# Slot transfers issued by piece, high pieces first, and the mask's halves exchanged behind them

## What is computed

```
x = x + L0_xattn(layernorm(x), ctx)        # 16 heads of width 8, rotary, no mask
x = x + L0_ffn(layernorm(x))               # ternary weights
x = x + L1_xattn(layernorm(x), ctx, mask)  # 16 query heads, 4 key heads, causal AND mask
x = x + L1_ffn(layernorm(x))               # 8 experts, the best one for each token
```

## Time and profile before

| | us |
|---|---|
| median of 3 runs | 588.3 (587.66 to 589.43) |
| the profiled execution, its own time | 586.95 |
| its span | 585.1 |
| PE busy in the span | 495.1 (85%) |
| DVE / ACT / POOL busy | 399.3 / 357.0 / 374.8 |

### The profile page before, as it was taken

One profiled execution on the slowest core, in us unless ns is written; L12 is line 12 of the kernel. 1 busy time (PEld: TensorE's weight loads), 2 busy tenths in 40 slices (PEclk: granted clock), 3 DMA queues, 4 the chain that ended last, 5 costly groups with the idle time before them and its releaser, 6 DMA issues.

```text
span 585.1 us, 20027 instructions
## 1 busy us (share of the span) xinstructions
PE 495.1 (85%) x6238; PEld 363.5 (62%) x6239; DVE 399.3 (68%) x1244; ACT 357.0 (61%) x872; POOL 374.8 (64%) x751
## 2 busy tenths in 40 slices
PE   3569898999988799988799999899998742999993
PEld 2346566666665589986455555555554422999992
DVE  7657777777798568644668888888878763444441
ACT  3227677777766555653566777677765652666661
POOL 6876666667673257675666688878887472445552
PEclk9999999999999999999999999999999985999998
DMA  5734334353432580004443455444554014334430
GB/s 165 184 76 125 90 92 118 85 126 87 119 89 64 193 226 1 1 2 111 118 111 89 104 134 137 128 103 111 133 138 110 26 56 143 80 96 104 101 94 27
DMA packets 102161, 59.92 MB, mean 102 GB/s; under 512 B 20338, under 2 KB 98178, under 8 KB 102098
## 3 DMA queue, kind: packets, MB, share of 16 engines
q1 hardware_dynamic: 98738, 51.79, 35.1%
q0 software_dynamic: 2784, 6.82, 3.4%
q10 hardware_dynamic: 576, 0.53, 0.3%
HBM read 19.90 MB, written 8.81 MB: 49 GB/s over the span
## 4 chain that ended last, share of the span: by engine, by line
PE 47%; SPq 14%; DVE 10%; DMA 10%; issue 10%; ACT 4%; POOL 3%; ACTq 1%; DVEq 0%; POOLq 0%
SPq L395 8%; DMA stack<-pieces 7%; PE bank L847 6%; PE bank L783 5%; PE bank L669 5%; PE scoreT L773 4%; DVE negmax L1408 4%; PE scoreT L835 4%; PE score L613 4%; PE bank L556 2%; PE score L835 2%; SPq L404 2%; PE bank L528 2%; PE scoreT L642 2%; PE bank L684 2%
## 5 line engine op out<-in xcount | busy, mean ns | idle before, releaser
L1408 DVE TENSOR_REDUCE negmax<-score 128x8 f32<-128x1024 f32 x128 | 156.2, 1220 | 35.4 <-PE score L613 24.9
L956 ACT ACTIVATE P<-scoreT 128x1024 f32<-128x1024 f32 x128 | 131.0, 1023 | 40.1 <-PE scoreT L633 21.7
L669 PE MATMUL bank<-P,Vc 128*32 128x128 f32 x2048 | 82.5, 279 | 1.9 <-DVE product L1516 1.5
L613 PE MATMUL score<-stack 64*128 64x128 bf16 x1024 | 62.7, 222 | 22.1 <-DMA stack<-pieces 13.1
L1312 POOL DMA_INDIRECT out<-by x39 | 40.2, 1031 | 50.6 <-DVE by L1715 48.0
L613 PEld LDWEIGHTS score<-stack 64*128 64x128 bf16 x1024 | 33.9, 95 | 48.7 <-issue 22.1
L669 PEld LDWEIGHTS bank<-P,Vc 128*32 128x32 f32 x2048 | 48.4, 109 | 15.8 <-issue 3.6
L962 ACT COPY outs<-bank 128x256 f32<-128x256 f32 x64 | 23.6, 369 | 49.8 <-PE bank L669 49.6
L1176 POOL TENSOR_TENSOR pieces<-full,pieces 128x256 bf16<-128x256 f32 x64 | 42.9, 670 | 14.4 <-ACT pieces L937 14.4
L1179 POOL TENSOR_TENSOR pieces<-rest,pieces 128x256 bf16<-128x256 f32 x64 | 43.8, 685 | 5.0
L847 PE MATMUL bank<-M,bhT 128*128 x312 | 43.5, 282 | 0.3 <-ACT bhT L1082 0.3
(11 more groups left out here) (211 smaller groups left out, 1265.7 us busy)
## 6 DMA issues: line engine op xcount, KB each, us to landing
stack<-pieces SPq DMA_DIRECT2D x192, 128.0 KB, 2.8
ctxT<-in_ctxT SPq DMA_DIRECT2D x32, 128.0 KB, 2.5
XB<-expert_rows SPq DMA_DIRECT2D x39, 66.0 KB
XA<-expert_rows SPq DMA_DIRECT2D x39, 64.0 KB
XR<-in_x SPq DMA_DIRECT2D x4, 512.0 KB, 4.5
stack<-blank SPq DMA_DIRECT2D x32, 64.0 KB, 2.1
stack<-negpT SPq DMA_DIRECT2D x64, 32.0 KB, 1.8
M<-in_M SPq DMA_DIRECT2D x1, 2048.0 KB, 9.9
```

The costliest lines, as they stand in the source:

```text
L613: mm = nc.tensor.matmul(SCORE[:, r, i * 128:(i + 1) * 128], Qs[pb][rows, h, tb * S:(tb + 1) * S], Ks[pb][rows, kv, tb * S:(tb + 1) * S], s ...
L669: mm = nc.tensor.matmul(PVOUT[VCOL * i:VCOL * (i + 1), half * 128:(half + 1) * 128], Vc[:, k % BODY, at:at + VCOL], P32[:, c, i * 128:(i + ...
L956: nc.scalar.activation(P32[:, half * 2:half * 2 + 2, :], SCORET[:], ACT.Exp, scale=SCALE).then_inc(sem("exp_done"), 1)
L1408: nc.vector.tensor_reduce(negmax[:, k % 2, :, half * HQ:(half + 1) * HQ], SCORE[:].rearrange("p r (h k) -> p r h k", h=HQ), AX.X, ALU.max, ...
```

## The change

`stack_both` waits by piece and sends the slots in the order 0, 1, 2, 4, 3, 5: slot 0 when both high pieces are there, slots 1, 2 and 4 when both middle pieces are, slots 3 and 5 when both low pieces are. `swap_mask` leaves the even step and stands in the odd one for the same pair (`j + 3`), behind `stack_both` and `max_rows` and ahead of `load_ctx` and `load_adj`. Nothing else is changed; the bytes moved and the number of transfers stay.

```diff
+SLOT_ORDER = (0, 1, 2, 4, 3, 5)
...
                 def stack_both(k):
...
-                        cut_q, cut_k = known(3 * (p + P0) + 3), known(3 * (p + P0) + 3)
-
-                        sp.wait_ge(sem("q_pieces"), cut_q)
-                        sp.wait_ge(sem("k_pieces"), cut_k)
-                        for s in range(SLOTS):
+                        high, middle, low = known(p + P0 + 1), known(3 * (p + P0) + 1), known(3 * (p + P0) + 3)
+
+                        sp.wait_ge(sem("q_high"), high)
+                        sp.wait_ge(sem("k_high"), high)
+                        for s in SLOT_ORDER:
+                            if s == SLOT_ORDER[1]:
+                                sp.wait_ge(sem("q_pieces"), middle)
+                                sp.wait_ge(sem("k_pieces"), middle)
+                            if s == SLOT_ORDER[4]:
+                                sp.wait_ge(sem("q_pieces"), low)
+                                sp.wait_ge(sem("k_pieces"), low)
                             sp.dma_start(rows_of(stack[b], s), both_pieces(b, s)).then_inc(sem(f"stacked{L}{b}"), 16)
...
                     max_rows(t + 1, j + 1)
                     if j % 2 == 1:
+                        if L:
+                            swap_mask(j + 3)
                         load_ctx(j + 7)
                         if L:
                             load_adj(j + 5)
-                    if L and j % 2 == 0:
-                        swap_mask(j + 4)
```

## The result

The changed kernel takes **599.1 us** (median of 4 executions, 595.74 to 607.11), the kernel before 588.9 beside it. The ratio is **1.0155, with a 95% interval of 1.0094 to 1.0217**. A second series gave 598.6 us and 1.0165 (1.0114 to 1.0217). So the change makes the kernel slower by 1.6%, some 9 us. The forecast was 594.1 us, with a range of 588.5 to 600.0.

The account below looks back on a forecast made before the run. Bound: the slot transfers, 8% of the span in SyncE's issue and 7% in flight, mostly in the second attention. Terms 5.6 + 0.5 + 0.2, less 0.5, give +5.8 us on 588.3: 594.1 us, range 588.5 to 600.

Parts of the forecast that it names:

- E: Second attention: start of a pair's first score matmul on PE, forecast 3.49 us behind the odd copy's end.
- the odd copy: The odd step's copy of the maxima on ACT (L972); E cannot come sooner than its end plus the queue behind it.
- The spacing of a pair: Second attention, E to E: 12.72 us per pair against 12.29, 13 x 0.43 = +5.6 us, because the halves are last.
- The landing: Second mask half, issue to arrival: taken as 2.0 us, with 1.8 and 2.8 kept as bounds.
- the prediction's own sign (9.14 to 9.3): Second attention: if the forecast is right, E to the odd copy's end stays at 9.14 to 9.3 us.
- No transfer that the change moves lies in it: Second attention, E to the odd copy's end: claimed to be compute only, mean 9.23 us, without transfers the change moves.
- The catch-up of 0.5 us: Taken off the sum: later pairs give POOL and DVE time, so the mean of 9.23 moves toward 9.14.
- The adjacency: Second attention, odd step: its load, issued later, delays DVE's mask in a few pairs; +0.5 us, bounds 0 and 6.5.
- the rival: The adjacency becomes the bound too: DVE waits for it in most pairs, half a us each; 600 us, chance 0.10.
- The slots, 1 to 1.4 us earlier: Second attention: slots land about 1.0 to 1.4 us earlier, so PE's wait of 0.95 to 1.19 us goes.
- The faster rival: Second attention: halves land in time and PE's slot waits go, all (581.5 us) or half (584.9); chance 0.10.
- The first attention: Only slot order and waits change: +0.2 us, bounds -2.7 and +1.5; spacing stays 10.0 us, first maxima at 28.4.

Follow-up runs that it names:

- one more issue ahead of the halves: Changed kernel with the mask halves issued one place later, behind the load of the context and ahead of that of the adjacency: 612.1 us, ratio 1.0402.
- the kernels with the halves out of the way: Slots by piece, halves at the end of the even step (585.1 us), ahead of the row of maxima in the odd step (586.5) or the even step (585.1).
- the halves last: Changed kernel with the mask halves at the end of the odd step, behind the loads of context and adjacency: 636.9 us, ratio 1.0768.
- the added matmuls: Kernel with the halves at the odd step's end, plus eleven matmuls per pair, result overwritten, while TensorE would wait for the halves: 627.3 us, ratio 1.0684.

## Why the prediction was right, and where its sizes were off

- **The mechanism** of the main cost is shown. The wait for the slots goes, the wait for the halves takes its place, and the halves alone, moved alone, make all of the loss (1.0179). Moved ahead of the row they make none. The chain, the lost wait for the slots and E at 3.33 us behind the odd copy are as forecast.
- **The spacing of a pair** was forecast at 9.23 + 3.49 = 12.72. The nine regular intervals have 12.68, but by two errors that cancel. From the odd copy's end to E it is 3.33 on the mean (3.24 to 3.54). The landing is what was too long: 1.85 us in the pair shown, where I took 2.0 by the transfer of equal size. The Trainium skill (DMA: Bandwidth & Descriptors, section Anatomy of one DMA — SWDGE (gpsimd) path) gives an estimate of 2.08 from its fit for another path; the measurement decides, and it is nearer to the median of the size in the earlier trace rows. From E to the odd copy it is 9.34 instead of 9.23, and 9.43 to 9.52 in most of the later pairs. By the prediction's own sign (9.14 to 9.3) this is a miss: 9 of the 13 intervals lie above 9.3, where 3 did before. "No transfer that the change moves lies in it" was wrong too, since the mask is made in that part, from the adjacency that the change moves back.
- **The catch-up of 0.5 us** had the wrong sign for these pairs: that part grew. Only with one more issue ahead of the halves is it the 9.14 I had expected.
- **The adjacency**, +0.5 us: DVE waits 1.0 us in 3 pairs for it, as foreseen, but bringing it forward by half a pair shows no gain. It does stand on the chain as the rival had it, but beside another way of nearly the same length, so the loss doesn't hang on it.
- **The four long intervals**, 6.6 us, are the term that was missing, and larger than the +5.0 of the spacing. In each the same two parts can be read. From the odd copy's end to E they have 4.34, 4.18, 5.42 and 3.41 us, together 4.0 more than 4 x 3.33: the first three are those with the long issue, and in the third the second half lands late as well. From E to the odd copy they have 10.69, 9.45, 9.45 and 10.37, together 2.6 more than 4 x 9.34: the first and the last are those with the low clock. The chain and the clock, each in the changed kernel:

```profile
446.45 3.92 DMA swapped<-mask
```

```profile
294.00:296.00 2.00, 2.00 (x24) 0.93 (x17) 1.52 (x3) 0.51 (x2) 1.04 (x2) 0.50 0.16 37
296.00:298.00 2.00, 2.00 (x14) 1.66 (x14) 0.98 (x4) 1.22 (x3) 0.00 (x0) 0.69 0.00 0
...
452.00:454.00 2.00, 2.00 (x24) 0.92 (x17) 1.50 (x3) 0.53 (x2) 0.00 (x0) 0.50 0.00 0
```

  I knew of landings of 3.70 us and kept them out of the mean. Long issues were in the trace of before too, where the slots' wait or the even step's slack hid them; I hadn't asked what they cost once the last transfer stands directly in front of E. And a PE wait was priced as its own length, without the step at half clock that can follow. For the first long interval even that isn't shown: its wait is 1.29 us, and at the same place in three other kernels waits of 1.28, 1.28 and 1.26 us were followed by a step at full clock.
- **Luck.** 599.1 us lies in the range up to 600, but the room above 594.1 was meant for a late adjacency (up to 6.5 us) and a slow landing. The long intervals filled it, and no term stood for them. The forecast was +5.8 us; the ratio stands for +9.1.
- **The slots, 1 to 1.4 us earlier:** true of their issue. In the pair at 359.23 the last of the six is issued 4.77 us behind the even copy's end, in the pair at 353.99 before it was 5.97. It is worth more than I gave it room for: alone this part is a gain of 0.75%. The faster rival (581.5 to 584.9) is nearly what the kernels with the halves out of the way reach (585.1 to 586.5), where its condition, halves that land in time, is met.
- **The first attention** stayed as forecast: the spacing is 10.0 us, and the first maxima start at 28.29 instead of 28.41, though PE's first scores start 0.46 us sooner (25.94, 26.40 before).

```profile
28.29 1.19 DVE L1415 TENSOR_REDUCE negmax<-score 128x8 f32<-128x1024 f32 x1
...
112.77 0.40 PE L620 MATMUL score<-stack 64*128 64x128 bf16 x8 [0.22 <-DVE negmax L1415]
...
122.79 0.40 PE L620 MATMUL score<-stack 64*128 64x128 bf16 x8 [0.22 <-DVE negmax L1415]
```

- **Open:** the 2.1 us from the last E to the end. In the other kernels, whose code there is the same, that stretch takes 132.7 to 136.3 us, without relation to what was changed. The kernel before has 132.5 in its one profile, at the lower edge. I take it for scatter between executions; that isn't shown.

## What to carry to other kernels

On a queue that works in order, a transfer's place is set by the last wait ahead of it, not by its size: put one that is ready early ahead of the wait for one that is late, and price a move by that wait plus the whole fixed time to landing. When a transfer becomes the last thing in front of TensorE, its rare slow cases count in full, and a wait of some 2 us can cost as much again in clock (here +3.0 us on a step of 5.87). Where a change has two parts, cost each alone: here one gained 0.75% and the other lost 1.8%.

## What the runs showed of the hardware

- **The clock follows waits of about 2 us, but not sharply.** Of the 17 first scores of a pair that came behind a wait of 2.19 us or more (in the seven profiles of kernels that wait for the halves and have no matmuls added), 16 were followed by a slow first step; the exception had waited 2.25. Of the 28 waits from 1.29 to 2.11 us, 11 were; of the 53 shorter ones none. So the length of that wait alone doesn't decide. With the halves last, in the five pairs from 355.15 to 423.01, the fall comes 1 to 2 us after PE has started again. The Trainium skill (TensorE: Matmul & The Clock Gate, section HAM oscillation — how this bites in real kernels) describes a kernel that waits for a transfer in each round and starts each round at the low clock. Those five pairs are such a case but for that delay, and the added matmuls, which took the clock from 0.84 to 1.00, agree.
- **Issuing a DMA can take longer than its neighbours by 0.4 to 1.2 us** (1.64 to 2.44 us for two instead of 1.24), and all ten cases in three profiles lie beside a transfer of the instruction queue.
- **A 32 KB transfer costs 1.7 to 1.9 us on the path** in the regular pairs of the changed kernel, 2.75 and 3.92 behind two of the long issues (304.96 and 446.45).
